# One-pass products of two-part operands in the grouped stage of a seven-layer kernel, and hand-written last turns

## The reference, cut to what matters

```python
qh = (q @ Wq.T).reshape(N, S_, 32, 8)          # q is x
kh = (k @ Wk.T).reshape(N, S_, 8, 8)           # k and v are the context
vh = (v @ Wv.T).reshape(N, S_, 8, 8)
...
attn = softmax(qh . repeat(kh, 4) / sqrt(8))
out = attn . repeat(vh, 4)
return out.reshape(N, S_, 256) @ Wfc.T + bfc
```

## Time and profile before

| | us |
|---|---|
| median of 3 runs | 2782.11 |
| lowest, highest | 2769.80, 2782.16 |
| the profiled execution, its own time | 2778.21 |
| its span, first to last instruction | 2776.4 |
| TensorE busy | 2629.9 |
| VectorE busy | 1911.3 |
| ScalarE busy | 1413.5 |
| GpSimd busy | 1183.0 |

### The profile page before, as it was taken

One profiled execution on the slowest core, in us unless ns is written; L12 is line 12 of the kernel. 1 busy time (PEld: TensorE's weight loads), 2 busy tenths in 40 slices (PEclk: granted clock), 3 DMA queues, 4 the chain that ended last, 5 costly groups with the idle time before them and its releaser, 6 DMA issues. The chain is left out here.

```text
span 2776.4 us, 66141 instructions
## 1 busy us (share of the span) xinstructions
PE 2629.9 (95%) x23860; PEld 2281.8 (82%) x23860; DVE 1911.3 (69%) x4152; ACT 1413.5 (51%) x3352; POOL 1183.0 (43%) x1559
## 2 busy tenths in 40 slices
PE   7999999996899999999999969998799999999995
PEld 7999999995798888888888858887577777777774
DVE  5655565555777777777777755444589999867775
ACT  3222222223666666666666643332466666666664
POOL 2211121113567767677677630112233444444443
PEclk9999999998999999999999989999799999999998
DMA  5000000001000000000000020000100000011110
GB/s 191 8 8 8 4 8 8 8 0 61 5 6 4 4 6 4 4 6 4 6 4 4 4 80 0 0 0 0 39 10 12 11 8 15 16 36 39 34 34 20
DMA packets 43394, 49.65 MB, mean 18 GB/s; under 512 B 3952, under 2 KB 33616, under 8 KB 43056
## 3 DMA queue, kind: packets, MB, share of 16 engines
q1 hardware_dynamic: 43312, 48.55, 5.4%
HBM read 35.96 MB, written 4.19 MB: 14 GB/s over the span
## 5 line engine op out<-in xcount | busy, mean ns | idle before, releaser
L588 POOL TENSOR_TENSOR a_probs<-a_probs,a_rs 128x512 f32<-128x512 f32 x64 | 70.5, 1102 | 467.0 <-DVE a_rs L444 467.0
L1174 POOL TENSOR_TENSOR b_rows<-b_rows,b_swapped 128x512 f32<-128x512 f32 x160 | 204.7, 1288 | 56.7 <-DVE b_swapped L947 56.7
L1109 ACT ACTIVATE b_probs<-bank,b_shift,b_q_scale 128x128 f32<-128x128 f32 x512 | 228.2, 461 | 0.6
L532 ACT COPY a_pT<-bank 128x512 f32<-128x512 f32 x64 | 37.5, 586 | 308.9 <-PE bank L325 308.9
L1221 POOL TENSOR_TENSOR b_probs<-b_probs,b_rs 128x512 f32<-128x512 f32 x128 | 133.2, 1040 | 138.6 <-DVE b_rs L999 135.5
L449 DVE TENSOR_TENSOR a_oT<-bank,a_oT 128x512 fp32r<-128x512 f32 x128 | 82.5, 686 | 144.6 <-ACT a_oT L537 144.4
L955 DVE TENSOR_REDUCE b_ss<-b_squares 128x4 f32<-128x512 f32 x192 | 125.2, 680 | 73.2 <-ACT b_squares L1084 73.2
L1184 POOL TENSOR_TENSOR b_rms<-b_rms,sh_minus_half 128x8 f32<-128x8 f32 (+1 forms) x128 | 170.4, 1331 | 10.6
L46 PE MATMUL bank<-a_xT,early_wq 128*128 128x256 f32 x512 | 150.6, 294 | 12.9 <-DVE early_wq L73 10.5
L46 PE MATMUL bank<-early_wo,b_oT 128*128 128x256 f32 x512 | 150.5, 294 | 1.4 <-DVE b_oT L921 1.4
L46 PE MATMUL bank<-early_wo,a_oT 128*128 128x256 f32 x512 | 145.6, 284 | 4.0 <-DVE a_oT L449 4.0
(11 more groups left out here) (386 smaller groups left out, 9058.1 us busy)
## 6 DMA issues: line engine op xcount, KB each, us to landing
d_x_in<-sh_x SPq DMA_DIRECT2D x32, 256.0 KB, 2.4
a_xT_in<-in_xT SPq DMA_DIRECT2D x16, 256.0 KB, 2.7
sh_x<-in_x SPq DMA_DIRECT2D x1, 4096.0 KB, 17.7
b_ctx_in<-in_ctxT SPq DMA_DIRECT2D x32, 128.0 KB, 2.0
e_cT<-in_ctxT SPq DMA_DIRECT2D x32, 128.0 KB, 2.5
out<-f_res SPq DMA_DIRECT2D x16, 256.0 KB, 2.5
a_qT<-in_L_attn_Wq SPq DMA_DIRECT2D x4, 512.0 KB, 6.1
a_stage<-in_L_attn_Wo SPq DMA_DIRECT2D x1, 2048.0 KB, 13.2
```

The lines of the kernel that those rows point to most:

```text
L1109: op = act.activation(probs[:, g % 2, keys], bS[:, keys], ACT.Exp, bias=shift[:, g % 2, a:a + 1], scale=q_scale[:, g, a // 2, a % 2:a % 2 ...
L1174: pool.tensor_tensor(rows[:, unit, :], rows[:, unit, :], swapped[:, half, :], ALU.add).then_inc(added[unit], 1)
```

## The change

- Keys, queries and the output product of the grouped stage are made by `product` from two parts each. The weights are split once in `from_first_to_second`: high parts on ScalarE (`g_high_w`), low parts on VectorE (`g_low_w`).
- Operands of a turn: the context is split on GpSimd (`g_split_context`, two operations). The rows are copied twice by ScalarE (`g_take_x`, a whole and a high part) and their low part is made on GpSimd (`g_low_x`). The attention's high part is ScalarE's copy as before, its low part is a new operation on VectorE (`g_low_att`).
- Waits go with it: `g_turn_x`, `f_turn_rows` and `g_project_out` wait on `g_att_low` instead of `g_att_taken`, `g_project_k` on `g_c_low`, `g_project_q` on `g_x_low`.
- GpSimd's pass stands one turn later against the others and holds two more steps.
- `from_first_to_second` has another order on all four engines.
- The last turns: `drain` is 1 (2 on GpSimd), and `last_turns` is an order written out by hand. `f_turn_rows`, `f_multiply`, `f_scale_rows` and `f_residual` can use other banks (`bS`) there.
- Tiles share memory with others that are no longer used. The value projection, scores, probabilities and the eight-bit product are as before.

```diff
@@ products and waits, TensorE @@
             def g_turn_x(i, oldest):
                 pe.wait_ge(x_loaded, nth(i.n, 1, 1, 16))
                 if oldest is not None:
-                    pe.wait_ge(g_att_taken, this(oldest))
+                    pe.wait_ge(g_att_low, this(oldest))
...
             def g_project_k(i):
-                pe.wait_ge(g_c_loaded, nth(i.n - n_turns, 2, 2, 16))
+                pe.wait_ge(g_c_low, this(i))
                 pe.wait_ge(g_x_taken, this(i))
                 for o in range(C):
                     for c in range(C):
-                        op = pe.matmul(bX[0][:, o * 256:(o + 1) * 256], g_wk[:, c, o * 128:(o + 1) * 128], g_cT[:, c, :],
-                                       start=(c == 0), stop=(c == C - 1))
+                        op = product(pe, bX[0][:, o * 256:(o + 1) * 256], parts(lambda a: g_split_k[:, a, c, o * 128:(o + 1) * 128]),
+                                     parts(lambda a: g_split_cT[:, a, c, :]), start=(c == 0), stop=(c == C - 1))
...
@@ VectorE @@
+            def g_low_att(i):
+                dve.wait_ge(g_att_taken, this(i))
+                dve.tensor_tensor(g_attT[:, 1], bX[0][:, :].rearrange("p (c n) -> p c n", c=C), g_attT[:, 0].bitcast(F32), ALU.subtract).then_inc(g_att_low, 1)
...
                 g_maximum(mid, 4)
                 g_shift(mid, 4)
                 g_shift(mid, 5)
+                g_low_att(old)
                 f_residual(older)
                 g_maximum(mid, 6)
...
@@ ScalarE @@
-                act.copy(g_xT[:, :, :], bX[0][:, :].rearrange("p (c n) -> p c n", c=C)).then_inc(g_x_taken, 1)
+                act.copy(g_x_whole[:, :, :], bX[0][:, :].rearrange("p (c n) -> p c n", c=C))
+                act.copy(g_xT[:, 0], bX[0][:, :].rearrange("p (c n) -> p c n", c=C)).then_inc(g_x_taken, 1)
...
@@ GpSimd @@
+            def g_split_context(i):
+                pool.wait_ge(g_c_loaded, nth(i.n - n_turns, 2, 2, 16))
+                hold(pool, sh.passed_pool)
+                pool.tensor_copy(g_split_cT[:, 0], g_cT[:, :, :]).then_inc(g_c_high, 1)
+                pool.wait_ge(g_c_high, this(i))
+                pool.tensor_tensor(g_split_cT[:, 1], g_cT[:, :, :], g_split_cT[:, 0].bitcast(F32), ALU.subtract).then_inc(g_c_low, 1)
+
+            def g_low_x(i):
+                pool.wait_ge(g_x_taken, this(i))
+                pool.tensor_tensor(g_xT[:, 1], g_x_whole[:, :, :], g_xT[:, 0].bitcast(F32), ALU.subtract).then_inc(g_x_low, 1)
...
             def g_turn(new, mid, old, oldest, older, eldest):
-                g_spread_k(new)
-                g_normalise(oldest)
-                g_add_bias(old)
-                f_deviation(older)
+                g_spread_k(mid)
+                g_normalise(older)
+                g_add_bias(oldest)
+                g_split_context(new)
+                f_deviation(eldest)
+                g_low_x(new)
...
@@ GpSimd, end of from_first_to_second @@
                 add_unit_att(d15)
+                g_split_context(e2)
                 residual(d15)
+                g_low_x(e2)
                 deviation(d15)
                 invert_deviation(d15)
                 scale_rows(d15)
+                g_spread_k(e2)
                 shift_rows(d15)
                 g_add_bias(e0)
-                g_spread_k(e2)
+                g_split_context(e3)
+                g_low_x(e3)
...
@@ TensorE, the end of the last turns @@
+            def last_turns():
...
+                for u in range(4, UNITS):
+                    pe.wait_ge(shifted[u], this(e15))
+                f_multiply(e13, None, None, bS[2])
+                g_weigh(e15, 6)
+                g_turn_probs(e15, 7, 6, False)
+                f_turn_rows(e14, None, None, bS[0])
+                g_weigh(e15, 7)
+                g_turn_att(e15, None, e13)
+                f_multiply(e14, None, None, bS[3])
+                pe.wait_ge(g_res_ready, this(e14))
+                g_project_out(e15, None)
+                f_turn_rows(e15, None, None, bS[1])
+                pe.wait_ge(g_res_ready, this(e15))
+                f_multiply(e15, None, None)
...
@@ VectorE, last_turns @@
+                g_take_att(e15, 1, 7)
+                f_round(e14)
+                g_low_att(e15)
+                f_residual(e14, bS[3])
+                f_moments(e14)
+                g_residual(e15)
+                g_moments(e15)
+                f_round(e15)
+                f_residual(e15)
+                f_moments(e15)
```

More of the change, by code:

```diff
@@ L2752, in _, with g_high_w @@
             act.copy(of_chunk[:, :, :], of_chunk_in[:, :, :]).then_inc(of_chunk_ready, 1)
+            def g_high_w(n):
+                whole, split = ((g_wk, g_split_k), (g_wq, g_split_q), (g_wo, g_split_o))[n]
+                act.wait_ge(g_w_loaded, 16 * sh.grouped.N_LOADS)
+                act.copy(split[:, 0], whole[:, :, :]).then_inc(g_w_high, 1)
             def g_take_x(i):
```

304 lines of the change are left out of this document (199 added, 105 removed).

## The result

| | before | after |
|---|---|---|
| median of 6 runs each | 2775.56 | 2802.81 |
| lowest, highest | 2769.80, 2782.16 | 2795.71, 2812.47 |
| the profiled execution, own time | 2778.21 | 2795.71 |
| its span | 2776.4 | 2793.9 |

The ratio is 1.009 with a 95% interval of 1.0071 to 1.0108: slower, and above the range that was forecast. TensorE's busy time has hardly changed (2629.9 to 2631.0 us); VectorE, ScalarE and GpSimd are busy 16, 11 and 50 us longer.

A forecast was written before the change was run, and what follows sets the result against it. TensorE, busy 95%, was taken as the bound, with a nearly as long VectorE chain beside it. Terms 6.4 + 0.3 + 0.3 + 4.4 - 0.6 + 0.7 - 9.0 = +2.5 us on 2778.2; forecast 2780, range 2758 to 2799.

The forecast's parts named there:

- The loop's stall: Grouped loop: x_in transposes wait for the attention's low part on VectorE, TensorE stands 1.45 us per turn; period 21.68 us.
- The saving of the products: Grouped loop, x_in transposes to next queries: three projections as two-part products save 0.87 us per turn.
- The rival of the clock: Grouped loop: the new hole lowers TensorE's clock behind the transposes, 11 turns lose 1.7 us each; 2799 us, chance 0.14.
- The gap of 1.34 us in the earlier trace: At 2724.83 us in the kernel before: left the clock full, taken as evidence against the falling clock.
- The transition: First stage to second: VectorE's idle time about covers its added work; +0.3 us, bounds -2 and +2.
- the second copy of e1's rows: ScalarE's additional copy of a turn's rows, 0.58 us, costed at nothing because ScalarE has waits there.
- The place where the loop begins: GpSimd spreads e2's keys before shifting d15's rows, so the first x_in transposes come late: +4.4 us.
- The last turns: After the loop: less waiting -0.6, more eight-bit steps +0.7, written-out order after the last weighing -9.0 us.

The follow-up runs named there:

- e3: Not a run: a turn of the grouped stage, its mark the first x_in transposes; its period's clock was 0.92, 0.88 and 0.88 in the changed kernel, 1.00 before.
- e4: Not a run: a turn of the grouped stage, without eight-bit work on VectorE; its period took 23.30, 23.26 and 26.31 us in the changed kernel.
- plain_all: Changed kernel with all three grouped-stage products in full precision from unsplit operands, every split and wait kept: 2807.7 us, ratio 1.0099.
- e15: Not a run: a late turn of the grouped stage; from its mark to the end 80.0, 80.0, 79.9 us in the changed kernel, 87.0, 88.9, 85.8 before.
- e0: Not a run: a turn in the transition to the grouped stage; d14's result is ready 21.06 us behind its mark in the changed kernel, 18.51 before.
- ffw_alone: Changed kernel with the feed-forward weights' rounding, combining and copy moved from d14's quantising to behind d15's: 2792.7 us, ratio 1.0055.
- e2: Not a run: a turn where the grouped loop begins; from its mark to the next turn's 14.9 us in the changed kernel, 10.3 before.
- rows_first: Changed kernel with GpSimd shifting d15's rows before it spreads the next keys: 2802.4 us, ratio 1.0057.
- ffw_last: Changed kernel with full-precision output product, no output-weight parts, d15's rows shifted before e2's keys, feed-forward weights' work behind d15's quantising: 2773.3 us, ratio 0.9996.

## Why the prediction was wrong

*The loop's stall* was right to 0.1 us: from the queries to the x_in transposes 10.36 us (2636.75 to 2647.11; 10.28 forecast), from there to the queries 11.42 (11.40), the low part right behind the two subtractions, and its removal takes it away. The saving of the products was right (0.89 for 0.87), and the period was 0.08 us longer than forecast, 1 us in all.

*The rival of the clock* was the first step that failed. I gave it eleven turns or none. It came in some turns, at 1.55 us each, and in the two turns ahead, whose periods grew by 1.9 to 2.7 (e3's, 19.23 before; +0.3 in the sum) and 1.9 to 5.0 us (e4's; +0.6 in the sum). The gap of 1.34 us in the earlier trace rows that left the clock full was taken as evidence for all gaps of that length; it was one gap at one place, and plain_all shows that the same hole can go either way with what stands around it. From e3 to e15 +13.6 where the sum has +6.7: of the 6.9 between them 4.5 lie in e3's and e4's periods, 1.5 in the later long ones.

*The transition* was the second, and about as large (6.2 us beyond its term): "VectorE has about as much idle time there as it gets work ... +0.3 (bounds -2 and +2)". It was +6.5, outside its bounds, 4.1 of it between e0 and e1. I balanced a sum of work against a sum of holes over the whole of the transition. What counts is one line: from the search for d14's largest value to its result VectorE has a chain, and the feed-forward weights stand inside it. The result came 2.55 us late: 1.3 from work ahead of the search, where the low part of the output weights (0.69 us by my price) took 2.15; 0.8 in the weights, where f_inner went from 0.41 to 2.09 us beside GpSimd's work while f_outer and f_w_twice lost their own stretch; 0.4 behind. Then came 1.5 us that no term had, the lower clock behind the long wait. ffw_alone, which only takes the feed-forward weights out, brings 5 us back of those two periods. From e1 to e2 1.5 us more were lost, beside a wait of 1.3 us for the second copy of e1's rows, which I had costed at nothing; no run takes that copy out. The page of the kernel before could have warned: TensorE already waited 0.6 us for that very result, so the chain had no slack.

*The place where the loop begins* was right as a sum (+4.6 for +4.4), but rows_first took only 1.7 us of it back: I had the low part of e0's attention as the end of the chain behind the late rows, and hadn't seen that it is a wait of its own when the rows are early.

*The last turns.* From the last weighing to the last product -10.0 (-9.0 forecast); but between e15's mark and that weighing 51.7 us against 48.8, where I had +0.1. Three steps of the eight-bit layer stand among the last weighings where one stood, and the clock of this stretch is 0.97 instead of 1.00, 1.6 us of full speed. In all -7.3 for -8.9.

*The quantised stage* had no term. A stage whose code doesn't change was taken as unchanged, and it moved by 6.6 us in the mean of the profiles; what moved it is open.

*The range* missed by 3.8 us because the transition's bounds were too narrow and because the clock's rival was added to the forecast's sum alone, with nothing going wrong beside it.

## What to carry to other kernels

A low part that is made on a busy engine and frees a bank is a new link in the turn: put its price against the saving of that one product, not of all of them, and place it right behind the copy that it needs. Where an engine's list leads through a chain (largest value, thresholds, result), count only the work inside the chain and look at what the other SBUF engine does at that time; holes elsewhere don't pay for it. Look at the clock behind a new long wait as well: here the same products cost 4.74 us in place of 3.19. And compare stages between marks in several profiles: here one stage of unchanged code spreads over 14 us (397.5 to 411.6), as much as 0.5% of the whole.

## What the runs showed of the hardware

*VectorE beside GpSimd.* Some of VectorE's operations that have all their operands in SBUF stretch until just after a GpSimd operation ends. In the changed kernel f_inner runs from 2398.92 to 2401.01, and GpSimd's product of rows, below, ends at 2400.72; with no GpSimd work beside it, once in the loop, it takes 0.42.

```profile
2399.69 1.03 POOL L3171 TENSOR_TENSOR sh_res<-sh_res,sh_rstd 128x512 f32<-128x512 f32 x1
```

In ffw_last f_w takes 2.14 us (0.69 alone) and f_w_twice 1.75 (0.29), the latter to 2443.10, with GpSimd's keys to 2442.95; the keys themselves took 4.54 in place of 3.75. In the loop f_fine has 1.21 us beside GpSimd and 0.43 in the one turn without, which bears out the reading of the earlier trace rows. Not every overlap stretches: f_inner, beginning together with a GpSimd operation, kept its 0.42 in the loop, and so did the residual's statistics (0.41). VectorE's operations with a bank among their operands kept their durations beside GpSimd (0.66 to 0.69 us on 128x512, 0.74 for f_res). The Trainium skill ("SBUF - State Buffer", on who interferes with whom) states this as an exclusive lock: a VectorE instruction with two inputs in SBUF, or in a two-port mode, and a GpSimd one that reads SBUF block each other for a whole instruction. These rows agree; that the effect moves with another engine's order, by up to 1.7 us an operation, I had not expected.

*The clock* fell to its lower level in the grouped loop in some turns and not in others of the same instructions and the same 1.37 us of idle time. The Trainium skill ("TensorE: Matmul & The Clock Gate", on psum-queue depth-cycling) says of another kernel that frequent small idle times between groups of matmuls make the clock oscillate. The changed kernel agrees in part (ten of 80 periods long over eight profiles), and plain_all shows that the idle time alone doesn't decide it.
